# An adapter and LoRA kernel: x of two batches loaded in halves, and one low part moved in VectorE's order

## The reference

```python
w = weight[adapter_ids]
y = jnp.einsum('bij,bkj->bik', x, w)
q = y[:, 107:-1, :].mean(axis=1)
routing = softmax(q @ router_W.T + router_b)
base = y @ W.T + b
t = jnp.einsum('bsd,erd->bser', y, A)
lora = jnp.einsum('bser,eor,be->bso', t, B, routing) * 2.0
out = x + base + lora
```

## Time and profile before

| | us |
|---|---|
| median of 3 timed runs | 72.85 (72.4 to 73.01) |
| the profiled execution, its own time | 72.17 |
| its span, first to last instruction | 70.5 |

### The profile page before, as it was taken

One profiled execution on the slowest core, in us unless ns is written; L12 is line 12 of the kernel. 1 busy time (PEld: TensorE's weight loads), 2 busy tenths in 40 slices (PEclk: granted clock), 3 DMA queues, 4 the chain that ended last, 5 costly groups with the idle time before them and its releaser, 6 DMA issues.

```text
span 70.5 us, 1142 instructions
## 1 busy us (share of the span) xinstructions
PE 65.9 (94%) x409; PEld 53.9 (76%) x409; DVE 43.0 (61%) x105; ACT 30.5 (43%) x62; POOL 1.2 (2%) x10
## 2 busy tenths in 40 slices
PE   2999989999999999999999999999999999999930
PEld 1332425743999988988988999888699999999920
DVE  1000022938999999779955999699554298250720
ACT  0800055487898993593036997300330330330000
POOL 5000000000000000000000000000000000000000
PEclk9999999999999999999999999999999999999999
DMA  0489999999999999999824014007230600600242
GB/s 0 112 265 384 358 387 409 417 405 414 409 407 412 407 409 405 409 409 402 333 64 104 9 42 107 0 0 298 47 88 19 151 3 9 284 14 0 69 154 74
DMA packets 7062, 15.30 MB, mean 217 GB/s; under 512 B 784, under 2 KB 3344, under 8 KB 7056
## 3 DMA queue, kind: packets, MB, share of 16 engines
q1 hardware_dynamic: 6624, 14.84, 56.2%
q10 hardware_dynamic: 432, 0.39, 2.1%
HBM read 12.08 MB, written 2.10 MB: 201 GB/s over the span
## 4 chain that ended last, share of the span: by engine, by line
PE 81%; DMA 8%; SPq 4%; issue 1%; DVE 1%
PE ps_o L556 32%; PE ps_t L556 8%; PE ps_o L573 8%; DMA wc_raw<-in_wcT_dram 8%; PE ps_y L516 5%; PE ps_y L539 4%; PE ps_y L538 4%; PE ps_y L540 4%; PE ps_yT L538 3%; PE ps_o L516 3%; PE ps_yT L540 3%; PE ps_yT L539 3%; PE ps_yT L549 3%; SPq L179 2%; SPq L184 1%
## 5 line engine op out<-in xcount | busy, mean ns | idle before, releaser
L556 PE MATMUL ps_o<-yT_hi,az_hi 128*128 128x256 f32 x64 | 18.1, 283 | 0.0
L556 PE MATMUL ps_o<-yT_lo,az_hi 128*128 128x256 f32 x64 | 17.8, 279 | 0.0
L556 PE MATMUL ps_o<-yT_hi,az_lo 128*128 128x256 f32 x64 | 17.8, 279 | 0.0
L556 PEld LDWEIGHTS ps_o<-yT_hi,az_hi 128*128 128x128 f32 x64 | 12.0, 188 | 0.1
L556 PEld LDWEIGHTS ps_o<-yT_hi,az_lo 128*128 128x128 f32 x64 | 12.0, 188 | 0.1
L556 PEld LDWEIGHTS ps_o<-yT_lo,az_hi 128*128 128x128 f32 x64 | 12.0, 188 | 0.0
L377 DVE TENSOR_TENSOR wc_lo<-wc_raw,wc_hi 128x1024 fp32r<-128x1024 f32 x10 | 11.9, 1211 | 0.1
L286 ACT CAST wc_hi<-wc_raw 128x1024 fp32r<-128x1024 f32 x10 | 10.0, 1052 | 0.0
L445 DVE SCALAR_TENSOR_TENSOR o_sb<-ps_o,rest_raw,xT_raw 128x256 f32<-128x256 f32 x16 | 7.1, 478 | 3.1 <-PE ps_o L573 3.1
L300 ACT ACTIVATE expd<-logit,nmax 128x8 f32<-128x8 f32 x8 | 2.3, 293 | 12.8 <-DVE nmax L427 12.8
L516 PE MATMUL ps_y<-wc_raw,xT_raw 128*128 128x512 f32 x16 | 7.4, 597 | 0.2 <-DMA wc_raw<-in_wcT_dram 0.2
(11 more groups left out here) (71 smaller groups left out, 111.9 us busy)
## 6 DMA issues: line engine op xcount, KB each, us to landing
wc_raw<-in_wcT_dram SPq DMA_DIRECT2D x16, 512.0 KB, 12.1
out_dram<-o_sb SPq DMA_DIRECT2D x3, 512.0 KB, 3.7
rest_raw<-in_rest_dram SPq DMA_DIRECT2D x2, 512.0 KB, 9.5
xT_raw<-in_xT_dram SPq DMA_DIRECT2D x2, 512.0 KB, 14.3
yT_raw<-y_turn SPq DMA_DIRECT2D x14, 64.0 KB, 2.1
xT_raw<-in_xT_dram SPq DMA_DIRECT2D x3, 256.0 KB, 6.7
out_dram<-o_sb SPq DMA_DIRECT2D x4, 128.0 KB, 1.9
rest_raw<-in_rest_dram SPq DMA_DIRECT2D x1, 278.0 KB, 7.6
```

Of the source, the lines that this page charges most:

```text
L556: last = mm(bank[:, 0:N2], stat[:, n, c, :], mov[pair][:, c].rearrange("p b s -> p (b s)"), start=(c == 0 and k == 0), stop=(stop and c == ...
```

## The change

x0 and x1 are each loaded as two halves of two chunks (128 KB, 1 KB per partition), with a semaphore for each half. ACT's queue issues only x0's first half; its second half goes on SP's queue between the halves of adapter 0, and x1's halves go one ahead of adapter 1's first half and one between its halves. PE waits for each half of x at chunk 0 and chunk 2. `hi_x1` waits for x1's second half alone. x2 and x3 are loaded whole, as before. On DVE the first low half of adapter 7 is taken from the head of the pass g = 2 and put in the pass g = 1 between finish(1, 2) and lo_yT(5); `lo_x(7)` keeps its place, its condition is only written differently. The host lays x out in memory to fit.

```diff
@@ -16,11 +16,11 @@
 CONSTS = 44
 
 
-def adapter_lora_kernel(nc, xT0, xT, ids, wcT, rest0, rest1, rest2, rest3, out):
+def adapter_lora_kernel(nc, xT0, xT1, xT, ids, wcT, rest0, rest1, rest2, rest3, out):
 
 
     _, _, _, C, S = xT.shape
-    ALONE = xT0.shape[0]
+    ALONE = 2 + xT1.shape[0]
     PAIRS = xT.shape[0] + ALONE // 2
     B = 2 * PAIRS
     D = C * P
@@ -98,7 +98,8 @@
         az_raw = [rest_raw[:, n:n + D] for n in az_at]
         b_raw = rest_raw[:, FIRST + D:SECOND]
 
-        x_in = [sem(f"x{b}_in") for b in range(ALONE)] + [sem(f"x_pair{g}_in") for g in range(ALONE // 2, PAIRS)]
+        x_half_in = [[sem(f"x{b}_in{n}") for n in range(2)] for b in range(2)]
+        x_in = [None] * 2 + [sem(f"x{b}_in") for b in range(2, ALONE)] + [sem(f"x_pair{g}_in") for g in range(ALONE // 2, PAIRS)]
         wc_in = [[sem(f"wc{b}_in{n}") for n in range(2)] for b in range(B)]
         rest_in = [sem(f"rest{n}_in") for n in range(4)]
         stored = [sem(f"stored{g}") for g in range(PAIRS - 1)]
@@ -185,8 +186,11 @@
                              wcT[bass.ds(a[b], 1), h].rearrange("a p c o -> (a p) (c o)"))\
                     .then_inc(wc_in[b][h], 16)
 
+            def load_x_half(b, h):
+                sp.dma_start(flat(xT_raw[:, b, half_of(h), :]), xT0[b, h]).then_inc(x_half_in[b][h], 16)
+
             def load_x(b):
-                sp.dma_start(flat(xT_raw[:, b]), xT0[b]).then_inc(x_arrived(b), 16)
+                sp.dma_start(flat(xT_raw[:, b]), xT1[b - 2]).then_inc(x_arrived(b), 16)
 
             def load_x_pair(g):
                 sp.dma_start(xT_raw[:, 2 * g:2 * g + 2].rearrange("p b c s -> p (b c s)"),
@@ -196,9 +200,11 @@
                 sp.dma_start(rest_raw[:, cols], rest).then_inc(rest_in[n], 16)
 
             load_wc(0, 0)
+            load_x_half(0, 1)
             load_wc(0, 1)
-            load_x(1)
+            load_x_half(1, 0)
             load_wc(1, 0)
+            load_x_half(1, 1)
             load_wc(1, 1)
             load_x(2)
             load_wc(2, 0)
@@ -287,7 +293,7 @@
                         .then_inc(wc_hi_ready, 1)
 
             def hi_x1():
-                act.wait_ge(x_arrived(1), 16)
+                act.wait_ge(x_half_in[1][1], 16)
                 copy(flat(xT_hi[1][:, HALF:]), flat(xT_raw[:, 1, HALF:])).then_inc(x1_hi_ready, 1)
 
             def hi_wc1(c):
@@ -308,7 +314,7 @@
                                          scale=rout[:, i:i + 1]).then_inc(tsT_hi_ready, 1)
 
             act.wait_ge(ident_ready, 1)
-            act.dma_start(flat(xT_raw[:, 0]), xT0[0]).then_inc(x_arrived(0), 16)
+            act.dma_start(flat(xT_raw[:, 0, half_of(0), :]), xT0[0, 0]).then_inc(x_half_in[0][0], 16)
             act.wait_ge(warm_ready, 1)
             nc.scalar.activation(junk[:], warm[:, 0:1], ACT.Exp)
 
@@ -468,7 +474,8 @@
             lo_wc(3)
             lo_az(4)
             for b in range(2):
-                dve.wait_ge(x_arrived(b), 16)
+                for h in range(2):
+                    dve.wait_ge(x_half_in[b][h], 16)
             finish(0, 0)
             finish(0, 1)
             lo_x(4)
@@ -481,7 +488,8 @@
                 ahead = 2 * g + 2 < B
                 router_parts(g)
                 if ahead:
-                    lo_wc(2 * g + 3, (0,))
+                    if g == 1:
+                        lo_wc(2 * g + 3, (0,))
                     turn(2 * g + 2)
                     lo_wc(2 * g + 3, (1,))
                 logits(g)
@@ -496,9 +504,11 @@
                     lo_yT(2 * g + 2)
                 for c in range(3):
                     finish(g, c)
+                if 2 * g + 5 == B - 1:
+                    lo_wc(2 * g + 5, (0,))
                 if ahead:
                     lo_yT(2 * g + 3)
-                if 2 * g + 4 < B:
+                if 2 * g + 5 == B - 1:
                     lo_x(2 * g + 5)
                 if g < PAIRS - 1:
                     finish(g, 3)
@@ -509,7 +519,9 @@
             mm = nc.tensor.matmul
 
             def y_raw(b, c, bank):
-                if c == 0:
+                if b < 2 and c % HALF == 0:
+                    pe.wait_ge(x_half_in[b][c // HALF], 16)
+                elif c == 0:
                     pe.wait_ge(x_arrived(b), 16)
                 if c % HALF == 0:
                     pe.wait_ge(wc_in[b][c // HALF], 16)
@@ -688,7 +700,8 @@
     bT = b.transpose(0, 2, 1).reshape(e * r, d)
     wcT = contraction_first(wc).reshape(-1, P, 2, c // 2, d).transpose(0, 2, 1, 3, 4)
     arrays = {
-        "xT0": xT[:4].reshape(4, P, c * s),
+        "xT0": np.ascontiguousarray(xT[:2].reshape(2, P, 2, c // 2 * s).transpose(0, 2, 1, 3)),
+        "xT1": xT[2:4].reshape(2, P, c * s),
         "xT": np.ascontiguousarray(xT[4:].reshape(-1, 2, P, c, s).transpose(0, 2, 1, 3, 4)),
         "ids": np.ascontiguousarray(np.asarray(itok_B_1_14).reshape(1, nb)),
         "wcT": np.ascontiguousarray(wcT),

```

## The result

The changed kernel is slower: median 73.05 us against 72.66 of the kernel before, 20 runs each, a ratio of 1.008 (95% interval 1.0056 to 1.0104), which is 0.4 to 0.8 us. The profiled execution has a span of 71.3 us, about 0.9 over the span of before (its own time is 73.07 against 72.17). One of the two parts did what was forecast and the other lost five times what was forecast.

What follows compares the result with a forecast made beforehand. PE bounds the kernel, with holes at loads before 10.15, batch 1's split products and batch 7's stalls. Order -0.45 plus loads +0.2 gives -0.25 us: median 72.6 against 72.85, no measurable change, faster side; range 71.9 to 73.2.

Steps and rivals of the forecast that it cites:

- the worst case of the loads alone: Loads of x and adapter 1: each half of x moves at 172 GB/s, adapter 1 1.4 us later, PE 1.3 us later.
- What bounds the kernel: Whole kernel: PE busy 65.9 of 70.5 us, with holes before 10.15, at batch 1's split products and batch 7's two stalls.
- DVE's order, gain 0.45: Batch 7's y on PE: moving adapter 7's first low part ahead of lo_yT(5) removes two stalls, gain 0.45 us, bounds 0.2 to 0.49.
- Adapter 0's second half, 0.42 us later, hidden in the hole before 10.15: Batch 0's y: half lands 0.33 to 0.42 us later, y(0) ends up to 0.3 later at 10.0, before PE's 10.15.
- Adapter 1's first half lands at 10.02 again: Start of batch 1's y: the same bytes stand ahead, so it lands at 10.02 and PE starts at 10.15.
- Adapter 1's second half, 0.38 late, PE loses 0.2: Batch 1's split products: load 0.38 us later, last weight load 0.35 late, PE loses 0.2 us.
- The best end of this part, a whole hole of 0.42 gained: Loads, before batch 1's y: if adapter 1 arrives earlier in both halves, PE's whole 0.42 us wait before 10.15 goes.
- Rival 2: Adapter 1's second half, then batch 1's split: small rows slow x's halves, PE loses 0.8 us, time 73.2; chance 0.12.

## Why the prediction was wrong

The range, 71.9 to 73.2, held the time, but the forecast was a small gain and the chip shows a loss. The range was narrower than the prediction's own bounds: the worst case of the loads alone (PE 1.3 us late) would have given 73.7. Point by point:

- *What bounds the kernel*: right. PE, behind the landing of adapter halves, then DVE at batch 7.
- *DVE's order, gain 0.45*: right. In the profile the pieces of batch 7's y from 49.84 to 52.68 take 2.84 us; before, the same pieces took 3.28, from 48.55 on the earlier trace rows, so 0.44. By the timed runs of this part alone it is 0.3, with 0.45 inside the interval.
- *Adapter 0's second half, 0.42 us later, hidden in the hole before 10.15*: this is the step that failed. It had landed at 7.58 before, 0.42 ahead of its product, so with 0.42 more it would indeed have been hidden. It landed at 9.25, 1.67 later, and PE took it up 1.39 after 8.0; less the hole of 0.42, that is about the 0.95 lost. The step priced a load as one piece, by the bytes ahead of it at the rate of its neighbours. Ten of its 16 shares were in by 7.91, within that price (7.58 + 0.42 = 8.0); the other six came from 8.29 to 9.25, and the last is the one waited for. The 33 kB loads show that what stands between the halves costs by its place: 0.7 us for one of them between adapter 0's halves.
- *Adapter 1's first half lands at 10.02 again*: wrong, from the same cause. The last share came at 10.91, 0.89 later, though the bytes ahead were the same. It cost nothing, since PE came to it only at 11.18.
- *Adapter 1's second half, 0.38 late, PE loses 0.2*: ACT's high part came at 12.57, 1.26 late and not 0.38, but as PE was itself 0.95 late, only 0.27 more were lost. The lateness was wrong by three times. That the loss came out near 0.2 is luck: two errors, the late half and the late PE, nearly cancel.
- *The best end of this part, a whole hole of 0.42 gained*: never near.
- *Rival 2 (slower, 73.2)* came out in time, and at a chance of 0.12 it was far too cheap. Its mechanism was wrong: small rows cost nothing that can be measured (0.9991, 0.9954 to 1.0027, with x1's halves together), and its place was adapter 1's second half, where the loss was mostly at adapter 0's. The Trainium skill's page "Perfetto Trace Analysis", section "DMA Optimizations", warns of small transfers under 2 KB; the halves together, and the kernel with x0's halves on ACT's queue, show no such cost at 1 KB rows. The section's next item, that splitting may help where DMA engines are generally idle, is not contradicted: they were not idle, and splitting did not help.

The sum had been -0.45 + 0.2; it was -0.3 to -0.45 for the order and +1.0 (0.6 to 1.5) for the loads. Why the packets behind the break are slow stays open, so the step is known, and its cause in the hardware is not.

## What to carry to other kernels

A load that is squeezed between two halves of a larger one is not priced by its bytes: measure it, with a load so small that its bytes can't matter. Where a first wait has only the room of a small hole (here 0.4 us), leave the stream that feeds it unbroken. And time parts that meet on different engines apart; here the gain of one hid a third of the loss of the other.

## What was not expected of the hardware

- One load of 33 kB between the two halves of the first adapter cost 0.7 us (1.0101), the same between the halves of the second nothing that could be told (1.0018). Where a profile shows it, the engines' share falls less than the rate: 0.79 at 239 GB/s over 2 us with the small loads, against 0.92 at 332 with them behind x1; 1.07 at 155 and then 0.40 at 76 with the change's loads alone, against 1.07 at 423 before. Why the packets behind such a break are slow wasn't tried and stays open.
- The 16 shares of a load do not finish together: the last came 0.30 us behind the first for the first half of adapter 0 before, 0.85 for the second half of adapter 1, and 1.85 for the half behind the change's break. A landing worked out from the mean rate misses this.
- Rows of 1 KB were as good as rows of 2 KB (0.9991, 0.9954 to 1.0027).
- The start of the first adapter's data varies from one execution to the next: PE began y(0) at 6.11 in the changed kernel, at 6.29 before, at 6.56 with the order alone and at 6.82 with x0's halves, though the loads ahead of it were issued alike but for the last, where SP's queue began 0.4 us later. Such a late start, 0.3 to 0.75 us behind the usual 2.76, stands in 6 of the 17 profiles. Four of them have a load between adapter 0's halves and two have not; whether that is chance is open, and how often it happens in the timed runs is not on record. Single profiles of these kernels differ by as much as the effects do, and only the timed runs decide.
